# Turning the experts' sums: two stacked unit matrices in place of transposes, and the end of the kernel in two halves

## The reference, cut to what matters

```
h = gelu(einsum('td,edh->teh', xf, W1) + b1)   # 8 experts, hidden size 128
y = einsum('teh,ehd->ted', h, W2) + b2
out = einsum('ted,te->td', y, mask)            # sum over the two chosen experts
return h3 + out                                # h3: the stage's input, before its norm
```

## Time and profile before

| | us |
|---|---|
| Median of 3 runs | 196.98 |
| The 3 runs | 197.11, 190.92, 196.98 |
| The profiled execution | 191.07 |
| Its span, first to last instruction | 189.4 |

### The profile page before, as it was taken

One profiled execution on the slowest core, in us unless ns is written; L12 is line 12 of the kernel. 1 busy time (PEld: TensorE's weight loads), 2 busy tenths in 40 slices (PEclk: granted clock), 3 DMA queues, 4 the chain that ended last, 5 costly groups with the idle time before them and its releaser, 6 DMA issues.

```text
span 189.4 us, 2093 instructions
## 1 busy us (share of the span) xinstructions
PE 138.8 (73%) x682; PEld 83.5 (44%) x682; DVE 127.1 (67%) x343; ACT 77.2 (41%) x126; POOL 31.6 (17%) x52
## 2 busy tenths in 40 slices
PE   0699959599960494699597233529999799979991
PEld 0382625227750212658486222526766355444430
DVE  6957895789499698999868899983330887012011
ACT  2010251436366431885752022335514365545541
POOL 3022210407105342342400232010000000000000
PEclk9999996957997558559969755585899999999999
DMA  5799934000000000000000000000000000002011
GB/s 142 268 394 362 398 134 114 0 0 0 0 0 0 0 0 0 3 2 2 0 0 3 2 0 0 0 0 2 0 3 0 0 0 3 0 0 55 0 28 28
DMA packets 7138, 9.20 MB, mean 49 GB/s; under 512 B 2388, under 2 KB 4436, under 8 KB 7128
## 3 DMA queue, kind: packets, MB, share of 16 engines
q1 hardware_dynamic: 7128, 9.07, 14.3%
HBM read 8.55 MB, written 0.52 MB: 48 GB/s over the span
## 4 chain that ended last, share of the span: by engine, by line
PE 43%; DVE 36%; DMA 7%; issue 5%; ACT 4%; SPq 3%; POOL 1%; DVEq 0%; ACTq 0%
PE bank L907 8%; DMA dist_sb<-in_dist 7%; PE bank L891 5%; PE bank L892 3%; PE bank L689 3%; DVE rs_a L957 2%; PE bank L778 2%; PE bank L704 2%; PE bank L662 2%; DVE st_sum L969 1%; PE bank L701 1%; PE bank L697 1%; PE bank L706 1%; DVE rs_v L966 1%; DVE dist_sb L1000 1%
## 5 line engine op out<-in xcount | busy, mean ns | idle before, releaser
L582 ACT ACTIVATE hid<-bank 128x512 f32<-128x512 f32 x32 | 18.0, 599 | 21.4 <-PE bank L892 21.3
L1284 DVE TENSOR_TENSOR h<-bank,h 128x256 f32<-128x256 f32 x4 | 1.7, 422 | 23.2 <-PE bank L917 23.2
L907 PE MATMUL bank<-hid,ffn_sb 128*64 128x512 f32 x64 | 16.8, 614 | 0.0
L891 PE MATMUL bank<-xp,w1hi 128*128 128x512 f32 x32 | 15.1, 473 | 0.4 <-ACT xp L566 0.4
L1198 DVE TENSOR_TENSOR dist_sb<-bank,early_sb 128x256 f32<-128x256 f32 x16 | 6.0, 419 | 10.3 <-PE bank L783 9.5
L892 PE MATMUL bank<-xp,w1lo 128*128 128x512 f32 x32 | 12.9, 402 | 0.0
L1000 DVE TENSOR_TENSOR dist_sb<-dist_sb,mask_in 128x1024 f32<-128x1024 f32 x8 | 9.4, 1220 | 4.3 <-POOL mask_in L331 4.3
L639 PE MATMUL bank<-dist_sb,neigh 128*64 128x512 f32 x32 | 10.3, 713 | 0.0
L891 PEld LDWEIGHTS bank<-xp,w1hi 128*128 128x128 f32 x32 | 6.3, 195 | 8.7 <-ACT hid L582 5.2
L674 PE MATMUL bank<-early_sb,x 128*128 128x128 f32 x8 | 1.7, 352 | 9.1 <-DVE gsum L1099 8.5
L778 PE MATMUL bank<-dist_sb 64*128 64x256 f32 x16 | 6.7, 506 | 2.2 <-DVE dist_sb L1198 2.0
(11 more groups left out here) (249 smaller groups left out, 352.9 us busy)
## 6 DMA issues: line engine op xcount, KB each, us to landing
dist_sb<-in_dist SPq DMA_DIRECT2D x4, 1024.0 KB, 10.9
mask_in<-in_mask SPq DMA_DIRECT2D x4, 256.0 KB, 10.1
ffn_sb<-in_ffn SPq DMA_DIRECT2D x1, 816.0 KB, 10.9
fold_sb<-in_folded SPq DMA_DIRECT2D x1, 772.0 KB, 12.4
late_sb<-in_late SPq DMA_DIRECT2D x1, 728.5 KB, 11.5
mask_in<-in_mrows SPq DMA_DIRECT2D x1, 512.0 KB, 3.6
out<-h SPq DMA_DIRECT2D x8, 64.0 KB, 1.7
early_sb<-in_early SPq DMA_DIRECT2D x1, 391.0 KB, 3.1
```

Source lines behind the costliest of these rows:

```text
L582: nc.scalar.activation(hid[:, at % HB], bank[hid_bank[at % 3]][:, :], ACT.Gelu).then_inc(S["hid_set"], 1)
L891: nc.tensor.matmul(o, w1hi[:, e * HID:(e + 1) * HID], xp1[g][:, toks], start=True, stop=False)
L907: mm = nc.tensor.matmul(bank[2][j * D:(j + 1) * D, :], K["e_w2"][:, (e + j) * D:(e + j + 1) * D], hid[:, (at + j) % HB], start=False, stop ...
```

## The change

It has four parts.

First, the turn. Each transpose of 128 by 128 becomes a product: the same piece of `y_t` is the stationary operand, and the moving operand is a new constant `ident2`, 128 rows by 64 columns, two unit matrices of 64 stacked. The product's value for a token and a feature is the sum of the even and the odd experts' sums, so it writes 64 columns per tile where the transpose wrote 128. There are 16 such calls, as before.

Second, the addition. DVE has one addition (the turned sum plus `h3`) per half where it had two.

Third, the end. For the last half (`g` and `k` both 1) ACT copies bank 2 in two pieces of 256 columns, PE turns two pieces after the first copy and two after the second (into two different banks), DVE adds 128 columns for each, and SP stores chunk 2 after the first and chunk 3 after the second, each by one transfer that holds both batches. `y_copied`, `yt_mm` and `y_set` each count one higher.

Fourth, the constant: `early` grows by 64 columns.

```
-         ("b2_rows", P, D), ("ident", P, P), ("tri", P, P), ("half_ones", P, NH_)]
+         ("b2_rows", P, D), ("ident", P, P), ("tri", P, P), ("half_ones", P, NH_), ("ident2", P, D)]
...
                 for k in range(2):
-                    sp.wait_ge(S["y_set"], 2 * g + k + 1)
-                    for f in range(NH_):
-                        sp.dma_start(out[2 * g + f, 2 * k * P:(2 * k + 2) * P].rearrange("(c p) d -> p c d", p=P),
-                                     h[:, g, 2 * k:2 * k + 2, f]).then_inc(stored, 16)
-            sp.wait_ge(stored, 2 * 16 * B)
+                    if g == 0 or k == 0:
+                        sp.wait_ge(S["y_set"], 2 * g + k + 1)
+                        for f in range(NH_):
+                            sp.dma_start(out[2 * g + f, 2 * k * P:(2 * k + 2) * P].rearrange("(c p) d -> p c d", p=P),
+                                         h[:, g, 2 * k:2 * k + 2, f]).then_inc(stored, 16)
+            for c in (2, 3):
+                sp.wait_ge(S["y_set"], c + 2)
+                sp.dma_start(out[NH_:2 * NH_, c * P:(c + 1) * P].rearrange("f p d -> p f d"), h[:, 1, c]).then_inc(stored, 16)
+            sp.wait_ge(stored, 16 * 2 * B)
...
-                    nc.scalar.copy(y_t[:, k], bank[2][:, :]).then_inc(S["y_copied"], 1)
+                    if g and k:
+                        for cols in (slice(0, 256), slice(256, 512)):
+                            nc.scalar.copy(y_t[:, k, cols], bank[2][:, cols]).then_inc(S["y_copied"], 1)
+                    else:
+                        nc.scalar.copy(y_t[:, k], bank[2][:, :]).then_inc(S["y_copied"], 1)
...
                     for c in range(4):
-                        mm = nc.tensor.transpose(bank[turn_bank[g] + k][:, c * P:(c + 1) * P], y_t[:, k, c * P:(c + 1) * P], ident)
+                        if g and k and c == 2:
+                            mm.then_inc(S["yt_mm"], 1)
+                            pe.wait_ge(S["y_copied"], 2 * g + k + 2)
+                            pe.wait_ge(S["y_set"], 2)
+                        i = turn_bank[g] + k if c < 2 or not (g and k) else turn_bank[0]
+                        mm = nc.tensor.matmul(bank[i][:, c * D:(c + 1) * D], y_t[:, k, c * P:(c + 1) * P],
+                                              K["ident2"], start=True, stop=True)
                     mm.then_inc(S["yt_mm"], 1)
...
                 def output(k):
-                    dve.wait_ge(S["yt_mm"], 2 * g + k + 1)
-                    yt = bank[turn_bank[g] + k][:, :].rearrange("p (c j d) -> p j c d", j=2, d=D)
-                    tiles = slice(4 * k, 4 * k + 4)
-                    link(nc.vector.tensor_tensor(v8(h[:, g])[:, tiles], yt[:, 1], v8(h3[:, g])[:, tiles], ALU.add))
-                    nc.vector.tensor_tensor(v8(h[:, g])[:, tiles], yt[:, 0], v8(h[:, g])[:, tiles],
-                                            ALU.add).then_inc(S["y_set"], 1)
+                    done = 2 * g + k + 1
+                    halves = ((0, 2), (2, 4)) if g and k else ((0, 4),)
+                    for a, b in halves:
+                        dve.wait_ge(S["yt_mm"], done)
+                        done += 1
+                        i = turn_bank[g] + k if a == 0 else turn_bank[0]
+                        yt = bank[i][:, 0:4 * D].rearrange("p (t d) -> p t d", d=D)[:, a:b]
+                        nc.vector.tensor_tensor(v8(h[:, g])[:, 4 * k + a:4 * k + b], yt, v8(h3[:, g])[:, 4 * k + a:4 * k + b],
+                                                ALU.add).then_inc(S["y_set"], 1)
...
-        "half_ones": (np.arange(P)[:, None] // D == np.arange(NH_)[None, :]).astype(f)})
+        "half_ones": (np.arange(P)[:, None] // D == np.arange(NH_)[None, :]).astype(f),
+        "ident2": np.tile(np.eye(D, dtype=f), (2, 1))})
```

## The result

| | the changed kernel | the kernel before |
|---|---|---|
| Median, 22 runs each | 193.57 us | 192.72 us |
| Lowest and highest | 191.54 and 197.16 | 190.15 and 197.11 |
| Ratio, 95% interval | 1.0092 [1.006, 1.0125] | |
| The same again, 12 runs against 34 | 1.0047 [1.0014, 1.008] | |

The change makes the kernel slightly slower: 0.9% in the first measurement, 0.5% in the second. I had forecast 197.6 us, 0.60 us over a median of 196.98, which is 0.3%. With 22 runs that median is 192.72: two of the three runs first shown were the two longest of the 22. The ratios leave out the slower runs of each kernel; the medians of all 22 runs each are 0.85 us apart, a ratio of 1.0044.

A forecast was written before the change was run, and what follows sets the result against it. PE was taken to carry the chain of waits without a break from 168 to 184.5 us. Inner turns +1.32, end -0.81 and constant +0.09 summed to +0.60 us on the median 196.98: 197.6 us, range 190.6 to 198.6.

The forecast's parts named there:

- The level: Whole kernel: base taken as the median 196.98 us, two of three runs being at 197; the lower level was 191.07 us.
- my own case: Whole kernel: the change adds 0.60 us, chance 0.60; 195.9 to 199.3 us at the upper level, 190.0 to 193.4 lower.
- The inner turns: Group 0's two turns and group 1's first: 12 more records of 0.11 us on PE's chain, +1.32 us.
- The end: From the last copy's start to the last store's issue: halves and one addition less move that issue by -0.81 us.
- the split earns little: Last half: most of the -0.81 us was put down to the addition saved and the second issue.
- The constant: Early table's load: 33 KB more at 364 GB/s delays the third distances, +0.09 us.
- Moving columns: Rival, all turns: cost follows moving columns, so inner turns cost nothing more; -0.96 us, 196.0 us or 190.1; chance 0.12.
- The clock, for better: Rival, experts' stretch: products keep PE's clock up, median falls to the lower level, 191.7 us, 2.7% faster; chance 0.14.
- A falling clock among group 1's experts: Rival, 168 to 184.5 us: 5 us of PE work falls to half clock, 202.6 us or 196.7; chance 0.08.
- A sign that I had named against myself: Changed kernel's trace: a granted clock under 1.00 between 134 and 186 us would prove the prediction wrong.
- Absorbed turns: Rival, inner turns: later weight loads or ACT hide the 1.32 us, only -0.72 stays, 196.3 us; chance 0.06.

The follow-up runs named there:

- the end with transposes: Against the kernel before: last half in two halves with two copies and merged transfers, transposes and both additions kept; ratio 0.9839, the second time 0.9986.
- the product alone: Against the kernel before: all four turns are products with one addition, end not split, new constant in the early table; ratio 1.0075.
- the end alone: Against the changed kernel: the three inner turns are transposes with two additions again, the last half stays changed; ratio to the kernel before 0.9968.
- the constant alone: Against the kernel before: 64 more columns in the early table, read by nothing; ratio 0.9993, the second time 0.9954.
- the turns four times over: The three inner turns repeated four times: as transposes in the kernel before, ratio 1.0199; as products in the product-only kernel, ratio 1.0424.

## Why the prediction was wrong

**The level: the step that failed.** "On the median it is 196.98 + 0.60." I took two of three runs for a sign of where the median falls and added the change to them. The forecast time was 4.03 us too long (197.6 against 193.57), and the base alone was 4.26 too long: 196.98, where 22 runs give 192.72. Nor are there just the two levels that I reckoned with: of those 22 runs 10 lie from 190.15 to 191.91 us, 8 from 192.66 to 193.46 and 4 from 195.64 to 197.11. That the measured time lies within 190.6 to 198.6 is owed to the range having been drawn over both levels; it lies between what my own case gave at the lower one (190.0 to 193.4) and at the upper one (195.9 to 199.3).

The traces show now where the level is made. The stretches view over the lead, columns as in the earlier trace rows, for the kernel before:

```profile
0.00:166.98 166.98, 121.24 (x608) 75.77 (x608) 123.81 (x335) 68.78 (x112) 31.59 (x52) 0.82 0.15 52
```

and for the changed kernel's first profile:

```profile
0.00:172.29 172.29, 124.76 (x608) 78.36 (x608) 124.00 (x335) 68.67 (x112) 31.36 (x52) 0.78 0.15 51
```

The records are the same 608, 608, 335; what differs is the granted clock, 0.82 against 0.78. Over all fourteen traces the lead was 166.0 to 168.0 us in the nine with a mean clock of 0.81 to 0.83 there, and 171.6 to 172.3 us in the five with 0.78 to 0.80. Both kinds occur with the constant and without it.

The difference sits in one stretch of PE's work. It runs from the second four records of line 655 to the second eight of line 662 (663 and 670 in the kernels with the new end); PE goes through some 30 records there without a gap. In the kernel before, in the changed kernel's first profile, and in the end with transposes, second time, which has neither the product nor the constant, it is

```profile
45.36:50.56 5.20, 5.20 (x30) 3.88 (x28) 2.98 (x6) 2.88 (x4) 0.97 (x1) 1.00 0.00 0
45.77:55.77 10.00, 10.00 (x29) 7.11 (x28) 3.04 (x6) 2.87 (x4) 0.88 (x1) 0.50 0.00 0
45.26:55.26 10.00, 10.00 (x30) 7.11 (x29) 3.05 (x6) 2.87 (x4) 0.88 (x1) 0.50 0.00 0
```

The same work takes 5.20 to 5.75 us in the nine traces with a short lead, at a granted clock of 0.90 to 1.00, and 9.37 to 10.00 us in the five with a long one, at 0.50 to 0.53. All the rest of the lead comes to 160.5 to 162.4 us in all fourteen, although its mean clock differs too: the same work behind this stretch, 51.00 to 134.89 us before and 56.44 to 140.22 us in the first profile, has 0.69 and 0.65 and takes 83.89 and 83.78 us. So here, where PE works without a gap, the lower clock costs nearly 5 us, and elsewhere in the lead it costs little; and the level is decided more than 100 us before the change's code is reached. What decides it no run shows: in both traces of the changed kernel PE had waited over 2 us for DVE just before this stretch (2.17 and 2.50 us), and one has the long lead and the other the short one.

**The size of the change: too low, and in part open.** The prediction put at nothing whatever the change might do outside its own pieces, the constant apart. In those pieces it was nearly right, as the next paragraphs show: 1.32 - 0.81 = +0.51 us forecast, +0.61 to +0.62 measured. The first ratio, 1.0092, is three times the forecast 1.0031; what stands in place of the nothing is under "The ratio" below, and its cause stays open.

**The inner turns, +1.32 us: right, slightly low.** Measured +1.41 (19.01 - 17.60; +1.43 in the first profile), and +1.40 and +1.41 in the kernels that share them. The difference is not in the turns' own pieces, 0.91 + 0.40 = 1.31 us, but behind them: the hidden product that follows a turn stands in the chain with 0.29 us where it had 0.23 after four transposes.

**The end, -0.81 us: right.** Measured -0.80; last issue 1.89 us after the copy's start, where I had 1.85. The first copy took 0.38 us (I took 0.37) and both together 0.65 (0.69), the turn 1.12 (1.05), the additions 0.29 (0.28). My remark that the split earns little was wrong: of the 0.80 us it is the split and the merged transfers that earn 0.68 to 0.69, by the kernel with transposes; the saved addition is paid for by the longer turn, by the kernel with the product alone. The two parts help each other only by 0.1 us.

**The constant, +0.09 us: neither shown nor refuted.** Two measurements gave 0.9993 and 0.9954, and the table landed about 0.1 us later with it, within the spread of both kinds.

**The ratio.** The forecast +0.60 holds 0.09 for the constant, which would act in the lead; without it the forecast is +0.51 against the +0.61 of the changed stretches, so that 0.60 and 0.61 agree so well is luck. 0.61 us is 1.0032, with 0.09 more it would be 1.0037. Of three measurements of kernels with these stretches, 1.0092, 1.0047 and 1.0038, all lie above it, and the intervals of the last two hold it. That the first one lies so far above is not explained by any part of the change that I could take out: the end alone, the product alone and the constant alone each came out near what their stretches say. The spread of the lead, 6 us between executions, is ten times the sum, and the medians of all 22 runs in the first measurement give 1.0044. I take the excess for a draw of the lead; it is not shown, and a small effect of the change on the lead isn't excluded.

**The rivals.** Moving columns: refuted by the turns four times over. The Trainium skill, "TensorE: Matmul & The Clock Gate", has the two rules that stood against each other; the weight load's ("LDWEIGHTS (loading the stationary operand)", an estimated 107 ns for 128 columns) agrees with 0.110 to 0.114 us per record, the isolated gap's 29 ns for 64 columns (section "Back-to-back issue gap") is not what these records show. The clock, for better: the time is far below the upper level, but so is that of the kernel before, so the products didn't bring it down. Products inside kept nothing up that transposes let fall, since with the transposes four times over, which are 5.4 us of the stretch from 168.5 to 184 us, the granted clock is still 1.00 there (columns as in the earlier trace rows):

```profile
168.50:184.00 15.50, 15.50 (x88) 9.51 (x86) 2.06 (x5) 5.53 (x10) 0.00 (x0) 1.00 0.08 18
```

A falling clock among group 1's experts was seen in no trace: in all fourteen the granted clock of the inner stretch is 1.00. A sign that I had named against myself, a clock under 1.00 between 134 and 186 us, did occur, 0.96 in the changed kernel's first profile and 0.99 in its second trace, but there the lower level ended before the inner stretch began; the sign was drawn too wide. Absorbed turns: none was.

## What to carry to other kernels

A transpose of 32-bit data on PE is one record and a plain 32-bit product is two, and at the upper clock, with 128 stationary columns and 128 moving columns or fewer, each record costs about 0.11 us. (The hidden products move 512 columns and take 0.23 us a record; their operands are declared `float32r`, and a call is one record, 32 calls and 32 records at line 891. No run tried the turn so.) Folding an addition into the turn cost time where PE alone carried the chain, gave nothing where turn and addition both stood in it (0.45 us more against 0.46 less), and gave 0.12 us where the longer turn ran beside the second copy. Judge each copy of a replaced step by its own place: the same swap cost 1.41 us in three places and gave 0.12 in the fourth. When the runs of a kernel are spread by more than the change is worth, take the base from many runs, and compare stretches of traces between fixed events.

## What the runs showed of the hardware

The inner stretch, all at the upper clock level, repeats to 0.01 us: 17.60 or 17.61 in each of the eight traces with transposes there once over. The end of one kernel repeats as well, to 0.02 us, while the lead of the same instructions varies by 6 us. Of PE's two clock levels, 1.2 and 2.4 GHz, the lower one cost very different amounts: some 30 records that PE works without a gap took 5.20 us at a granted clock of 1.00 and 10.00 us at 0.50, which makes the short and the long lead, while the 84 us behind them took the same time at 0.69 and at 0.65.

In the two traces of the end with transposes, additions on DVE of 128x128 from PSUM start 0.32 us apart when one waits for the other and 0.21 us apart when not, at 0.29 us each.
